# Four banks for the last head's units, an earlier start of head 0's units, and another order at a mixer's end

## The reference, cut to what matters

```python
mod = (_silu(c) @ wmod).reshape(1, 6, 1, -1)            # for each block
h = _layernorm(x) * (1 + ca) + sa
# block 0, attention
scores = einsum('bhgtd,bhkd->bhgtk', qg, k) / sqrt(DH)   # q, k rotated; causal
attn = softmax(where(causal, scores, min))
x = x + ga * (einsum('bhgtk,bhkd->bhgtd', attn, v) @ Wo.T)
...
# block 1, mixer
h = gelu(h @ w_down.T + b_down); xmid = h
h = _hydra(_hydra(h))            # each ends in y * rsqrt(mean(y*y) + 1e-5) * norm_w @ out_w.T
h = xmid + alpha * xmid + (1 - alpha) * h
x = x + ga * (h @ w_up.T + b_up + h_in)
# block 1, gated layer
x = x + gb * lora(silu(lora(h, w1)) * lora(h, w3), w2)
```

## Time and profile before

| | us |
|---|---|
| median of 3 runs | 752.07 (750.55 to 754.78) |
| the profiled execution, its own time | 754.48 |
| its span, first to last instruction | 752.7 |
| PE busy, share of the span | 711.7 (95%) |
| DVE busy | 472.8 (63%) |
| ACT busy | 318.0 (42%) |
| POOL busy | 314.6 (42%) |

### The profile page before, as it was taken

One profiled execution on the slowest core, in us unless ns is written; L12 is line 12 of the kernel. 1 busy time (PEld: TensorE's weight loads), 2 busy tenths in 40 slices (PEclk: granted clock), 3 DMA queues, 4 the chain that ended last, 5 costly groups with the idle time before them and its releaser, 6 DMA issues.

```text
span 752.7 us, 10280 instructions
## 1 busy us (share of the span) xinstructions
PE 711.7 (95%) x3718; PEld 429.2 (57%) x3718; DVE 472.8 (63%) x716; ACT 318.0 (42%) x536; POOL 314.6 (42%) x254
## 2 busy tenths in 40 slices
PE   4998899999999999889999999999979999999998
PEld 1444333433333342148787888654548788877886
DVE  3787677788888886236865557788875433338211
ACT  3311266667677777751325401463343223223100
POOL 0325673755566565771447333226322212125300
PEclk9999799999999999999999999999989999999999
DMA  8347516252260200330013200204100111011111
GB/s 308 106 127 224 123 44 166 73 123 48 78 123 18 39 3 9 94 99 28 29 57 98 71 0 1 77 30 87 70 0 1 57 56 55 29 56 59 41 70 43
DMA packets 24111, 53.00 MB, mean 70 GB/s; under 512 B 4252, under 2 KB 8100, under 8 KB 23044
## 3 DMA queue, kind: packets, MB, share of 16 engines
q1 hardware_dynamic: 24068, 52.44, 24.6%
HBM read 45.63 MB, written 6.60 MB: 69 GB/s over the span
## 4 chain that ended last, share of the span: by engine, by line
PE 79%; DVE 10%; issue 4%; DMA 2%; ACT 2%; SPq 2%; POOL 1%; DVEq 0%; ACTq 0%; POOLq 0%
PE ps L869 76%; DVE mxp L1812 2%; DMA rq<-in_mask 1%; PE ps L886 1%; DVE st L1654 1%; DVE xnb L1678 1%; ACT pr L1458 1%; PE ps L1053 1%; DVE rt L1693 1%; PE ps L1121 0%; SPq L719 0%; DVE x L1896 0%; DVE qsw L1863 0%; DMA q_parts<-parts 0%; POOL arena L2357 0%
## 5 line engine op out<-in xcount | busy, mean ns | idle before, releaser
L869 PE MATMUL ps<-arena 128*128 128x512 f32 (+1 forms) x1404 | 326.3, 392 | 1.9 <-DVE arena L1697 1.2
L869 PEld LDWEIGHTS ps<-arena 128*128 128x128 f32 (+1 forms) x1404 | 259.4, 186 | 60.4 <-DVE arena L1697 1.9
L1812 DVE TENSOR_REDUCE mxp<-ps 128x2 f32<-128x1024 f32 (+3 forms) x160 | 172.8, 1115 | 44.2 <-PE ps L869 43.6
L1458 ACT ACTIVATE pr<-ps 128x512 f32<-128x512 f32 x288 | 162.0, 596 | 75.5 <-PE ps L869 71.6
L869 PE MATMUL ps<-Qst,Kst 99*128 99x512 bf16 x288 | 100.2, 389 | 6.1 <-ACT pr L1458 4.8
L869 PE MATMUL ps<-Kst,Qst 96*128 96x512 bf16 (+3 forms) x384 | 98.3, 333 | 5.4 <-DVE mxp L1812 4.2
L2258 POOL TENSOR_TENSOR pr<-pr,cap 128x512 int32<-128x512 int32 x56 | 71.1, 1284 | 38.0 <-ACT pr L1458 38.0
L869 PE MATMUL ps<-pr,vr 128*32 128x512 f32 x576 | 76.5, 604 | 0.0
L869 PEld LDWEIGHTS ps<-Qst,Kst 99*128 99x128 bf16 x288 | 24.4, 98 | 79.6 <-ACT pr L1458 64.0
L869 PEld LDWEIGHTS ps<-Kst,Qst 96*128 96x128 bf16 x384 | 36.4, 99 | 51.3 <-DVE mxp L1812 20.2
L2357 POOL TENSOR_TENSOR arena<-raw,arena 128x1024 fp32r<-128x1024 f32 x11 | 26.2, 2391 | 81.0 <-ACT arena L1532 80.2
(11 more groups left out here) (203 smaller groups left out, 833.6 us busy)
## 6 DMA issues: line engine op xcount, KB each, us to landing
wmr<-in_wmr SPq DMA_DIRECT2D x8, 1280.0 KB, 10.6
raw<-in_w SPq DMA_DIRECT2D x16, 512.0 KB, 3.2
Qst<-q_parts SPq DMA_DIRECT2D x42, 128.0 KB
q_parts<-qparts SPq DMA_DIRECT2D x3, 768.0 KB, 4.9
x<-in_x SPq DMA_DIRECT2D x8, 256.0 KB, 5.9
wm<-in_wm SPq DMA_DIRECT2D x4, 512.0 KB, 7.5
raw<-in_up SPq DMA_DIRECT2D x8, 256.0 KB, 2.6
raw<-in_down SPq DMA_DIRECT2D x8, 256.0 KB, 2.6
```

What stands on the lines that cost most here:

```text
L869: return nc.tensor.matmul(outp, lhs, rhs, start=start, stop=stop, skip_group_check=True)
L1458: A(pr[:, k % PRING, :], ps[:, 4 + k % 2, :], ACT.Exp, scale=float(DH) ** -0.5).then_inc(exp_done, 1)
L1812: V.tensor_reduce(mxp[:, kh, g0:g0 + heads, i].rearrange("p (b e) -> p b e", e=per), units, AXX, ALU.max)\
```

## The change

Three places are written in another order, and the last head gets other banks and another mask.

```diff
-         ("lora", 0, 0), ("out", 1, 0), ("fd", 1, 1), ("scale", 1, 0), ("out", 1, 1), ("up", 0, 0), ("up", 0, 1),
-         ("scale", 1, 1), ("up", 1, 0), ("up", 1, 1)]
+         ("lora", 0, 0), ("out", 1, 0), ("fd", 1, 1), ("scale", 1, 0), ("out", 1, 1), ("up", 0, 0), ("scale", 1, 1),
+         ("up", 0, 1), ("up", 1, 0), ("up", 1, 1)]
...
+BEFORE_BODY = 3
+FIRST_AT = (1, 3, 5, 7, 8, 9, 10, 12, 13, 14, 15, 17, 18, 19, 20, 22, 23)
+SWAP2_AFTER, SWAP3_AFTER = 2, 7
...
-        todo += [(SCORES_AT[s - AHEAD], "s", 1, s) for s in range(AHEAD, NS)]
+        if ctx:
+            todo += [(SCORES_AT[s - AHEAD], "s", 1, s) for s in range(AHEAD, NS)]
+        else:
+            todo += [(FIRST_AT[s - BEFORE_BODY], "s", 1, s) for s in range(BEFORE_BODY, NS)]
...
+LAST_RING = (4, 5, 1, 3)
+def t_ring(n):
+    return LAST_RING if n == NKV - 1 else LAST_RING[:2]
...
+def masked_by_pe(n):
+    return n < POOL_MASKED or n == NKV - 1
...
-                if k >= 2 or n:
+                ring = t_ring(n)
+                if len(ring) > 2 and k == 2:
+                    pe.wait_ge(s_read, slots_before(n, NS))
+                if k >= len(ring):
+                    pe.wait_ge(exp_done, n * NTU + k - len(ring) + 1)
+                elif n and k < 2:
                     pe.wait_ge(exp_done, n * NTU + k - 1)
-                o = ps[:, 4 + k % 2, :].rearrange("p (g t) -> p g t", g=G)
-                by_pe = i == j and n < POOL_MASKED
+                o = ps[:, ring[k % len(ring)], :].rearrange("p (g t) -> p g t", g=G)
+                by_pe = i == j and masked_by_pe(n)
...
-            for s in range(AHEAD):
+            for s in range(BEFORE_BODY):
                 if s < 2:
                     queries(3, 1, range(2 * s, 2 * s + 2))
                 s_unit(1, s)
-            for b in range(4, 8):
+            for b in range(4, 6):
                 pe.wait_ge(read_b[b], banks.attn[b])
...
-                for r in range(ROUNDS):
-                    mask_round(n, r)
+                if not masked_by_pe(n):
+                    for r in range(ROUNDS):
+                        mask_round(n, r)
```

More of the change, by code:

```diff
@@ L128 @@
              ("fd_first", 1, 0), ("scale", 0, 1), ("fd_second", 1, 0), ("rest", 0, 1), ("merge", 0, 0),
-             ("gate", 1, 1), ("dg", 1, 0), ("fd", 1, 1), ("scale", 1, 0), ("up", 0, 0), ("dg", 1, 1),
-             ("up", 0, 1), ("scale", 1, 1), ("norm", 0, 0), ("up", 1, 0), ("up", 1, 1)]
+             ("gate", 1, 1), ("dg", 1, 0), ("fd", 1, 1), ("scale", 1, 0), ("dg", 1, 1), ("up", 0, 0),
+             ("scale", 1, 1), ("up", 0, 1), ("norm", 0, 0), ("up", 1, 0), ("up", 1, 1)]
 MIXER_POOL = [("out", 0, 0), ("wup", 0, 0), ("shift", 0, 0), ("out", 0, 1), ("shift", 0, 1), ("out", 1, 0),
@@ L328 @@
 assert len(SCORES_AT) == NS - AHEAD and len(AHEAD_AT) == AHEAD
+BEFORE_BODY = 3
+FIRST_AT = (1, 3, 5, 7, 8, 9, 10, 12, 13, 14, 15, 17, 18, 19, 20, 22, 23)
+SWAP2_AFTER, SWAP3_AFTER = 2, 7
+assert len(FIRST_AT) == NS - BEFORE_BODY and BEFORE_BODY == SWAP2_AFTER + 1
 assert SCORES_AT[CTX_AT - AHEAD - 1] < CONTEXT_AT < SCORES_AT[CTX_AT - AHEAD]
@@ L1035, in pv_round @@
                         pe.wait_ge(o_copied, 2 * n)
+                    else:
+                        for b in range(6, 8):
+                            pe.wait_ge(read_b[b], banks.attn[b])
                 pe.wait_ge(exp_done, n * NTU + 4 * r + 4)
-                if n >= POOL_MASKED and DIAG[r]:
+                if not masked_by_pe(n) and DIAG[r]:
                     pe.wait_ge(masked, masks_by_gpsimd(n, r))
@@ L1457, in head_body @@
                         act.wait_ge(pv_done, n * ROUNDS + (k - PRING) // 4 + 1)
-                    A(pr[:, k % PRING, :], ps[:, 4 + k % 2, :], ACT.Exp, scale=float(DH) ** -0.5).then_inc(exp_done, 1)
+                    A(pr[:, k % PRING, :], ps[:, t_ring(n)[k % len(t_ring(n))], :], ACT.Exp, scale=float(DH) ** -0.5).then_inc(exp_done, 1)
             for n in range(NKV):
@@ L1848, in head_body @@
                 for k, (_, what, d, s) in enumerate(body_steps(nxt, nxt2, ctx)):
-                    if n == 0 and k == 2:
-                        swap_queries(3)
                     if what == "s":
                         s_unit(n + d, s)
+                        if n == 0 and d == 1 and s == SWAP3_AFTER:
+                            swap_queries(3)
                     elif what == "max":
@@ L1870, in _ @@
             maxima(0)
-            for s in range(AHEAD):
+            for s in range(BEFORE_BODY):
                 s_unit(1, s)
-                if s == AHEAD // 2 - 1:
+                if s == SWAP2_AFTER:
                     swap_queries(2)
```

## The result

The changed kernel took 744.96 us (median of 6 executions, 743.63 to 747.66) against 752.67 us (6 executions, 750.55 to 754.78): a ratio of 0.990, 95% interval 0.9873 to 0.9928. That is 7.7 us less; the forecast was 743.5 us, from a sum of 9.5 us. The profiled execution took 743.63 us, and the two profiles are 10.9 us of span apart, more than the medians are. The experiments say why.

A forecast was written before the change was run, and what follows sets the result against it. PE, busy 95% of the span, bounds the kernel; only its waits or lower clock could give much. 4.6 + 3.7 + 1.2 = 9.5 us off 754.48 gives 745.0, median-adjusted 742.6; forecast 743.5, range 740.0 to 749.

The forecast's parts named there:

- Rival 1: Whole kernel: all three parts work and head 0's clock stays up; 743.5 us, 741 to 746; chance 0.60.
- the signs that the prediction named: Profile marks in last head, head 0 and mixer, such as the maxima's turn at 105 to 107 us, or contrary ones.
- Head 0, 3.7 us: Head 0: units moved behind three score units gain 1.1 us, the clock staying up 2.6; bounds 0 and 5.7.
- keeping the clock up: Head 0: PE busy some 85% of 80.1 to 84.5 us avoids the half clock, worth 2.6 us.
- Last head, 4.6 us: Last head: four banks remove ACT's gaps, 5.0 us, less 0.7 for masks, plus 0.25; bounds 0 and 5.3.
- ACT becomes the bound: Last head: with four banks ACT's 2.17 us per round exceeds PE's 1.97, so seven gaps of 0.72 us can go.
- The 2.40 for a round with two masks: Last head, rounds 1 to 3: PE needs 1.97 + 0.43 = 2.40 us, starving ACT for at most 0.7 in all.
- booked as a gain of 0.25: Last head: the last pv round follows the last exp at once instead of queuing second, gaining about 0.25 us.
- Mixer, 1.2 us: Mixer's end: an earlier `dg` and `hof` bring `rt` to 556.9 from 558.09, gaining 1.2 us; bounds 0 and 2.5.
- DVE is late next: Mixer's end: DVE, not PE, limits next, so the gain is 1.2 us, not PE's 4.14 us standstill.
- rival 3: Four banks give half, 746 us, or the mixer's new standstill lowers the gated units' clock, costing 3.4, 746.9; chance 0.10.
- the fourth rival: Head 0: clock stays at 0.50 up to the maxima's turn, at 122.5; slower, 759 us; chance 0.04.

The follow-up runs named there:

- the mixer alone: The kernel before with only the mixer's new DVE order added; 751.94 us, ratio 0.998.
- with GpSimd's masks: The changed kernel, four banks kept, with the last head's eight diagonal units masked by GpSimd again instead of TensorE; 746.91 us, ratio 0.9939.
- the kernel whose GpSimd waits: The changed kernel with GpSimd holding the last four steps of the third queries' rotation until head 1's maxima are split; one execution, 744.53 us.

## Why the prediction was right, and where it was off

**Right.** Rival 1 came true: all three parts act, head 0's clock stays up, and the time lies 1.5 us over the forecast, within its own range of 741 to 746. By the signs that the prediction named: the clock is 1.00 from 80 to 95 us and the turn comes at 105.42 (105.8 forecast); the four tiles run at full clock behind `hof`; the standstill moved to the transposes, 3.01 us; no wait for Wo; the last pv round alone. Two signs came out otherwise. ACT's idle time is 0.34 us in the masked rounds, not at most 0.25. And the clock does fall in front of the gated units, which was named as a sign of being wrong; in the profile it cost nothing, but in three profiles of related kernels a later fall cost 1.2 to 1.5 us. That the time came within 1.5 us is in part luck: 743.5 was chosen between 742.6 and 745.0 without a row that said so, and the last head's term came out by errors that offset each other.

**Head 0, 3.7 us.** In the profile 3.6, and its division holds: 1.1 for the order, 2.5 for the clock (2.6 said). What failed is the step from one execution to the median: "keeping the clock up" is earned only where the old order loses the clock, in an estimated 27 of 64 executions. The profiled execution of before was one of them. The sum was made against its 754.48, and the lower median was subtracted from the result, not taken as a sign that a term of the sum would shrink with it.

**Last head, 4.6 us.** Measured 4.9, but by other terms. "ACT becomes the bound" was wrong: the 2.17 us for four exps were those of two banks, where an exp waits for a unit that waits for its bank. With four banks PE is busy all the time, and ACT follows it: its 20 exps in 10.14 us are about the five rounds as PE sends them, one of 2.18 (with one mask) and four of 1.97. PE is the bound at the 1.97 us that the prediction had for it, so an unmasked round gained 2.89 - 1.97 = 0.92 instead of 0.72, and the masks cost PE their full time. The 2.40 for a round with two masks is what the trace shows (302.02 to 304.43). The seven rounds between the first and the last but one pv round fell from 20.24 (306.30 to 326.54) to 14.86 (302.02 to 316.88), 5.4 us. The last pv round, booked as a gain of 0.25, is a loss of 0.7: it no longer shares a wait, but from the round before it to the context's turn there are now 3.45 us for 2.73. The head's start gained 0.3. 5.4 - 0.7 + 0.3 is about 4.9. The prediction moved the masks for Wo's sake; the runs show that GpSimd cannot keep all eight because the pv rounds then wait for them, and that it can keep four.

**Mixer, 1.2 us.** Measured 1.6 against the one profile. Against the other profiles with the old order it is 0.7 to 1.2 (their `rt` stands 17.62 to 18.11 us behind the first tile), because the four late tiles took 5.26 to 5.93 us there, not 6.54: again one execution's clock. "DVE is late next" held, and the experiment that puts two additions into DVE's idle 1.41 us won 1.2 of them. The part of rival 3 that had the clock fall for the units behind the new standstill is partly true: not the 3.4 us of its price, but 1.2 to 1.5 us, in three of six profiles.

**The sum for the median.** With these figures the parts give an estimate: 2.2 in head 0 less the 0.3 given back, 4.9 in the last head, 0.7 to 1.2 in the mixer, 7.5 to 8.0 us in all, less the clock's second fall in the executions that have it. Measured are 7.7.

**The clock.** In the last head, from its unit 0 to the context's turn, the granted clock is 1.00 in all fourteen profiles. Five of them have two banks there, where PE stands still in every round (0.47 us in the earlier trace rows), and in a sixth PE waits three times for GpSimd's masks, up to 1.28 us; in the others it hardly stands still. The Trainium skill, "TensorE: Matmul & The Clock Gate", section "A second HAM failure mode: psum-queue depth-cycling", has the clock swing where PE cycles through PSUM banks with brief standstills; these six profiles do not agree. It tells of swings between the levels; a clock that stays at 0.50, as in the fourth rival, was the prediction's own reading of it, and no run shows that either. Where the clock did fall, PE had been half idle (head 0, busy for 1.95 of 4.45 us; the attention output with the mixer alone, 1.61 of 3.00; behind the transposes with GpSimd's masks, 2.65 of 5.00) or had stood still for 3 to 4 us (mixer). The same order of work also ran without a fall in other profiles: head 0's old order with the mixer alone, the new standstill with GpSimd's masks, the attention output in all the others.

## What to carry to other kernels

A stretch at 1.2 GHz in one profile is one execution's: look at the mean clock of every execution before its price goes into a forecast of the median, and at a second profile, since the mean does not say where the clock fell. Where only a ring of PSUM slots limits an engine, the time of its instructions in that trace can hold the wait for a slot too, and with more slots another engine may set the pace: find its round first. A standstill that is moved may lower the clock at its new place. A few spare matmuls there show what it costs, if they do not delay the work behind them.

## What was not expected of the hardware

DVE's short operations stood still while GpSimd worked. Timelines of DVE and POOL in the changed kernel:

```profile
103.58 1.23 DVE L1844 TENSOR_REDUCE mxp<-ps 128x2 f32<-128x1024 f32 x1 [0.43 <-PE ps L893]
104.84 0.43 DVE L1850 TENSOR_TENSOR nm<-mxp 128x32 f32<-128x32 f32 x1
...
106.47 2.25 DVE L1858 TENSOR_TENSOR mt<-mt,mparts 32x128 f32<-32x128 f32 x1
...
103.11 2.12 POOL L2252 TENSOR_TENSOR qacc<-qacc,qparts 128x1024 f32<-128x1024 f32 x1
...
106.44 2.14 POOL L2252 TENSOR_TENSOR qparts<-qacc,qparts 128x1024 bf16<-128x1024 f32 x1
```

The same in the kernel whose GpSimd waits:

```profile
104.57 0.19 DVE L1850 TENSOR_TENSOR nm<-mxp 128x32 f32<-128x32 f32 x1
...
105.78 0.28 DVE L1858 TENSOR_TENSOR mt<-mt,mparts 32x128 f32<-32x128 f32 x1
```

`mt` began 0.03 us behind GpSimd's operation and ended 0.14 behind its end: 2.25 us for 0.28. In the kernel before, GpSimd was done with these steps when the maxima came:

```profile
107.11 2.14 POOL L2220 TENSOR_TENSOR qparts<-qacc,qparts 128x1024 bf16<-128x1024 f32 x1
...
109.37 0.19 DVE L1818 TENSOR_TENSOR nm<-mxp 128x32 f32<-128x32 f32 x1
...
110.58 0.28 DVE L1826 TENSOR_TENSOR mt<-mt,mparts 32x128 f32<-32x128 f32 x1
```

By moving the maxima 3.6 us forward against the start, the change set them beside GpSimd's last steps, which gave 0.3 us back. DVE's reduction from PSUM beside GpSimd's operation took 1.23 us, as it did before the change. The Trainium skill, "SBUF — State Buffer", section "Who interferes with whom", says that a DVE instruction with two inputs in SBUF contends with a GpSimd instruction that reads SBUF, and that such contention is an exclusive lock; the trace agrees.

The clock falls at more places than the page of one execution shows: in the profile of the mixer alone the attention output's transposes ran at a mean of 0.66 (328 to 333 us) and took 5.38 us, where all other profiles show 3.71. What decides between executions of one order stays open.
